# Score tiles of four heads on 32 rows, two token tiles to a unit, in three attention layers of a fused decoder (Trainium2, 1 core)

## What is computed

```python
h = (x - mean(x)) / sqrt(var(x) + eps)          # per token
q, k, v = h @ Wq + bq, src @ Wk + bk, src @ Wv + bv   # src is h (a1) or the context (x2, x3)
s = einsum('bhqd,bhkd->bhqk', q, k) / sqrt(8)   # 16 heads of width 8, 64 x 64 scores
w = softmax(s)                                  # x3: the denominator has one more term, exp(0)
x = x + (w @ v) @ Wo + bo                       # x3 has no Wo
```

## Time and profile before

| what | value |
|---|---|
| median of 3 runs | 2318.76 us (2318.24 to 2321.27) |
| profiled execution, its span | 2356.9 us; no other time is given for it |
| phase a1 | 728.9 to 908.2 us of the span |
| phase x2 | 1453.9 to 1618.7 us |
| phase x3 | 1897 to 2061 us |
| busy over the span | PE 1774.8 us, DVE 1337.8 us, ACT 1099.5 us, POOL 746.9 us |

### The profile page before, as it was taken

The page is one execution under the profiler, slowest core; times in us unless marked ns, Lnnn a source line. Parts: engine busy times, 40 slices in busy tenths (PEclk is TensorE's granted clock), DMA queues, the critical chain, the costliest instruction groups (busy, mean ns, idle before and its releaser), DMA issues. The chain is left out here.

```text
span 2356.9 us, 39525 instructions
## 1 busy us (share of the span) xinstructions
PE 1774.8 (75%) x14484; PEld 1215.4 (52%) x14484; DVE 1337.8 (57%) x3646; ACT 1099.5 (47%) x2273; POOL 746.9 (32%) x718
## 2 busy tenths in 40 slices
PE   3887553999895996767999386887788868743994
PEld 1555432435543664644798253565555535542774
DVE  3897587502123774654343365885369969862223
ACT  4775531223243775733344243774357657610441
POOL 1223201360354331146255002330223232165453
PEclk9888885798896998877999697998979969955997
DMA  4111361125623301102376200000000010011224
GB/s 158 83 83 82 104 235 45 49 75 150 161 70 132 124 2 50 37 30 85 110 238 201 75 1 27 28 20 10 3 1 2 2 37 28 11 49 60 62 81 138
DMA packets 145170, 173.18 MB, mean 73 GB/s; under 512 B 21073, under 2 KB 120593, under 8 KB 144049
## 3 DMA queue, kind: packets, MB, share of 16 engines
q1 hardware_dynamic: 125252, 129.09, 17.7%
q0 software_dynamic: 13248, 28.21, 3.6%
q10 hardware_dynamic: 6480, 13.37, 1.5%
HBM read 126.84 MB, written 79.05 MB: 87 GB/s over the span
## 5 line engine op out<-in xcount | busy, mean ns | idle before, releaser
L1154 PE MATMUL a_AV<-a_vx,a_pT 128*64 128x18 f32 (+1 forms) x3072 | 115.1, 224 | 33.0 <-DVE a_two L824 15.3
L1154 PEld LDWEIGHTS a_AV<-a_vx,a_pT 128*64 128x64 f32 x3072 | 105.9, 146 | 62.2 <-issue 28.6
L1016 ACT ACTIVATE a_e<-a_e 128x512 f32<-128x512 f32 x192 | 110.2, 622 | 58.7 <-DVE a_e L846 58.5
L1141 PE MATMUL a_TP<-ident,a_e 128*128 128x128 f32 x768 | 108.0, 285 | 20.0 <-ACT a_e L1016 19.4
L1021 ACT COPY a_pT<-a_TP 128x512 f32<-128x512 f32 x192 | 103.4, 588 | 39.6 <-PE a_TP L1141 39.4
L846 DVE TENSOR_TENSOR a_e<-a_S,a_mx 128x1024 f32<-128x1024 f32 x96 | 117.3, 1222 | 2.9
L1141 PEld LDWEIGHTS a_TP<-ident,a_e 128*128 128x128 f32 x768 | 89.2, 146 | 57.6 <-ACT a_e L1016 48.3
L1130 PE MATMUL a_S<-a_kbd,a_qT 64*64 64x512 f32 x768 | 113.8, 668 | 0.9 <-issue 0.6
L3620 POOL DMA_INDIRECT f_back<-f_ys,f_row x78 | 74.7, 957 | 97.5 <-DVE f_ys L3709 85.6
L3126 POOL DMA_INDIRECT f_back<-f_ys,f_row x80 | 76.6, 957 | 87.1 <-DVE f_ys L3287 66.9
L3759 ACT ACTIVATE f_h<-f_H,f_wt 128x256 f32<-128x256 f32 x156 | 65.2, 473 | 83.5 <-PE f_H L3835 83.5
(11 more groups left out here) (544 smaller groups left out, 4731.4 us busy)
## 6 DMA issues: line engine op xcount, KB each, us to landing
f_wt<-in_f_ew SPq DMA_DIRECT2D x39, 584.0 KB
f_slots<-in_blank SPq DMA_DIRECT2D x1, 18576.0 KB
f_wt<-in_f_leaf SPq DMA_DIRECT2D x94, 98.0 KB, 2.0
f_xs<-f_slots SPq DMA_DIRECT2D x47, 144.0 KB
memory_x_k<-w_stage ACTq DMA_DIRECT2D x24, 256.0 KB, 3.2
f_slots<-in_blank SPq DMA_DIRECT2D x1, 5760.0 KB
f_xs<-leaf_slots SPq DMA_DIRECT2D x22, 256.0 KB
leaf_out<-f_ys SPq DMA_DIRECT2D x22, 256.0 KB
```

The source lines that it names most:

```text
L1016: act.activation(eh, eh, ACT.Exp).then_inc(weights.sem, 1)
L1141: last = pe.transpose(TP[:, half, P * n:P * n + P], ev[:, 4 * half + n, :], k.ident[:, :])
L1154: last = pe.matmul(AV[64 * c:64 * c + 64, 2 * hp * W1:2 * (hp + 1) * W1], pT[:, hp, 64 * c:64 * c + 64], vx[:, g % 2, t, c, 2 * hp:2 * hp ...
```

## The change

A new function `attention_pairs` takes the place of `attention` in a1, x2 and x3; a0 and a3 keep the old one. Its program for VectorE puts `shift_mean(g + 2)` between the shifts of an even pair (in x3 `update` too) and `update` between those of an odd pair; behind the second shift stand `take_v(g + 1)` (even) and `norm_sums(g + 3)` (odd). Further:

- `score` uses 32 rows (four heads) in place of 64: eight matmuls per tile of 256 columns in place of four of 512, each of the four row strips r into its own bank.
- A score unit is two tiles (a pair p) and takes four banks, so there is one unit in place of two. `score(p + 1)` waits for both shifts of pair p.
- `highest` is one reduction of 2048 scores for two tiles; `shift` and `exps` stay per tile.
- The block-diagonal keys hold four heads per strip in place of eight, and GpSimd spreads all of them, in four instructions per group. ScalarE spreads none.
- `weigh` of both tiles of a pair writes one `AV` bank, and `take_values` takes both with one reciprocal and one product.

```diff
-    kbd = ph.sb("kbd", [P, 2, 2 * GT, 8, SL])
-    S = ph.ps("S", [P, 2, 2, 512])
+    kbd = ph.sb("kbd", [P, 2, 2 * GT, HR, SL])
+    S = ph.ps("S", [P, NR, 2, HR * SL])
...
+            def spread_keys(n):
+                wait_keys(pool, n)
+                if n >= 2:
+                    pool.wait_ge(scores.sem, scores.after(2 * (n - 2) + 1))
+                shape = [P, 2, HR, SL]
+                kb_ = keys(n).rearrange("p (b j) -> p b j", j=SL)
+                for b in range(0, 2 * GT, 2):
+                    last = pool.tensor_tensor(kbd[:, n % 2, b:b + 2, :, :], bc(kb_[:, b:b + 2, :], 2, shape),
+                                              mask4[:, :].unsqueeze(1).unsqueeze(3).to_broadcast(shape), ALU.mult)
+                last.then_inc(kbd_ready.sem, 1)
...
+            def shift(p, t):
+                if p:
+                    v.wait_ge(turned.sem, 2 * (2 * (p - 1) + t) + 2)
+                v.tensor_tensor(e[:, t, :, :].rearrange("p (r h) j -> p r h j", r=NR), S[:, :, t, :].rearrange("p r (h j) -> p r h j", j=SL),
                                bc(mx[:, p % 2, :, t, :], 3, [P, NR, HR, SL]), ALU.subtract).then_inc(shifted.sem, 1)
...
+            for p in range(NPR):
+                highest(p)
+                shift(p, 0)
+                if p:
+                    take_values(p - 1)
+                between(p)
+                shift(p, 1)
+                behind(p)
...
+            def score(p):
+                g, h = p // 2, p % 2
+                if h == 0:
+                    pe.wait_ge(q_ready.sem, q_ready.after(g))
+                    pe.wait_ge(kbd_ready.sem, kbd_ready.after(g))
+                if p:
+                    pe.wait_ge(shifted.sem, shifted.after(2 * (p - 1) + 1))
+                for t in range(2):
+                    for c in range(2):
+                        b = 4 * h + 2 * t + c
+                        for r in range(NR):
+                            rows = slice(32 * r, 32 * r + 32)
+                            last = pe.matmul(S[64 * c:64 * c + 64, r, t, :], qT[rows, g % 2, SL * b:SL * b + SL],
+                                             kbd[rows, g % 2, b, :, :], start=True, stop=True)
+                last.then_inc(scores.sem, 1)
...
+            for p in range(NPR):
+                g, later = p // 2, p // 2 + 2 < NG
+                turn(p, 0)
+                if p + 1 < NPR:
+                    score(p + 1)
+                weigh(p, 0)
+                if p == 0 and not cross:
+                    make_v(1)
+                elif p % 2 == 0 and g and finishing:
+                    ...
+                    turn_att(g - 1)
+                elif p % 2 and later:
+                    make_q(g + 2)
+                turn(p, 1)
+                if p % 2 == 0 and g and finishing:
+                    project(g - 1)
+                elif p % 2 and later and not cross:
+                    make_k(g + 2)
+                weigh(p, 1)
+                if p % 2 == 0 and later:
+                    if g and finishing:
+                        pe.wait_ge(x_updated.sem, x_updated.after(g - 1))
+                    ...
+                    turn_x(g + 2)
+                elif p % 2 and later and not cross:
+                    make_v(g + 2)
...
-            3: lambda: attention(nc, k, d, "a1", ...
-            7: lambda: attention(nc, k, d, "x2", ...
+            3: lambda: attention_pairs(nc, k, d, "a1", ...
+            7: lambda: attention_pairs(nc, k, d, "x2", ...
-           10: lambda: attention(nc, k, d, "x3", ...
+           10: lambda: attention_pairs(nc, k, d, "x3", ...
```

More of the change, by code:

```diff
@@ L3876, in shape_tables @@
     t["ident"] = np.eye(P, dtype=f)
+    t["mask4"] = ((p[:, None] // 8) % 4 == np.arange(4)[None, :]).astype(f) * f(8.0 ** -0.5)
     t["mask8"] = ((p[:, None] // 8) % 8 == np.arange(8)[None, :]).astype(f) * f(8.0 ** -0.5)
@@ L4035, in decoder @@
             0: lambda: attention(nc, k, d, "a0", "a0_q", "a0_k", "a0_v", "a0_o", width=16, diff=0.8 - 0.6 * 2.718281828459045 ** (-3.6), fill="f1"),
-            3: lambda: attention(nc, k, d, "a1", "a1_q", "a1_k", "a1_v", "a1_o", qb="a1_bq", kb="a1_bk", vb="a1_bv", ob="a1_bo", fill="f3"),
-            7: lambda: attention(nc, k, d, "x2", "x2_q", "x2_k", "x2_v", "x2_o", kv="ctx", qb="x2_bq", kb="x2_bk", vb="x2_bv", ob="x2_bo"),
+            3: lambda: attention_pairs(nc, k, d, "a1", "a1_q", "a1_k", "a1_v", "a1_o", qb="a1_bq", kb="a1_bk", vb="a1_bv", ob="a1_bo", fill="f3"),
+            7: lambda: attention_pairs(nc, k, d, "x2", "x2_q", "x2_k", "x2_v", "x2_o", kv="ctx", qb="x2_bq", kb="x2_bk", vb="x2_bv", ob="x2_bo"),
             9: lambda: attention(nc, k, d, "a3", "a3_q", "a3_k", "a3_v", "a3_o", qb="a3_bq", kb="a3_bk", vb="a3_bv", ob="a3_bo",
                                  affine=("a3_ga", "a3_be"), bias=True),
-            10: lambda: attention(nc, k, d, "x3", "x3_q", "x3_k", "x3_v", kv="ctx", qb="x3_bq", kb="x3_bk", vb="x3_bv",
+            10: lambda: attention_pairs(nc, k, d, "x3", "x3_q", "x3_k", "x3_v", kv="ctx", qb="x3_bq", kb="x3_bk", vb="x3_bv",
                                   restricted=True),
```

387 lines of the change are left out of this document (added).

## The result

The changed kernel takes 2350.45 us (median of four runs, 2345.37 to 2355.28) against 2320.02 (four runs, 2318.24 to 2330.38; the fourth came after the forecast): a ratio of 1.0117, 95% interval 1.0086 to 1.0147, so about 27 us slower. The forecast was 2341, in a range of 2294 to 2364, with 0.63 on slower.

What follows compares the result with a forecast made beforehand. TensorE was taken to bound a1 and VectorE x3. The shorter loop wins 12 + 5 + 5 = 22 us, clock falls lose 44: 22 us slower, put on the median as 2341 us, range 2294 to 2364.

Steps and rivals of the forecast that it cites:

- Score: TensorE in a1, x2, x3: a pair's score burst takes 1.05 us in place of 2 x 1.02; bounds 1.0 and 2.04.
- Maxima and values: VectorE, per pair: reduction of 2048 scores 2.3 us, reciprocal about 0.3, product 0.33; about 0.5 us saved.
- Loop at the full clock: Group lengths at unchanged clock: a1 16.8 us against 19.19, x2 16.8 against 17.79, x3 16.5 against 17.80.
- shift_mean 0.2: VectorE in a1's odd pair: shift_mean was counted at 0.2 us within a VectorE sum of 1.97.
- Clock: TensorE's clock falls in the new loop's long waits; PEclk by phase about 0.95 (a1), 0.90 (x2), 0.78 (x3).
- Price of a fall: Time lost to the low clock: a1 7 us (2 falls of 3.4), x2 15, x3 22, together 44 us.
- 5.5 more: x3: a group wholly at the low clock costs TensorE about 22.0 us against 16.5, so 5.5 us more.
- The ends: First group and drain of a1, x2, x3: 0, 0 and +1.5 us, bounds -3 and +4 in each.
- Slow strips: Rival: score's row strips do not run beside each other, 2.04 us a pair; 38 us slower, 2357; chance 0.10.
- The clock holds: Rival: no clock falls in the new loop, so 22 us faster, 2297 (2304 with up to two falls); chance 0.27.
- Nothing to see: Rival: clock falls and loop gain cancel within 5 us, 2319; chance 0.10.
- x3 longer, x2 a little longer, a1 shorter: Sign named for the forecast: x3 longer than its 163 us, x2 a little longer, a1 shorter than 179.

Runs made afterwards that it cites:

- the moved turn_x: Changed kernel with values taken behind both shifts and turn_x put behind the odd pair's score, no idle matmuls: 2289.49 us, ratio 0.9868.
- both fillers: Changed kernel plus idle matmuls ahead of each score burst and ahead of turn_x (in x3 after an odd pair's second weigh): 2314.55 us, ratio 0.9978.
- the runs: The change in a1 alone, x2 and x3 as in the kernel before: 2323.92 us, ratio 1.0014.
- the doubling: Changed kernel with every score matmul issued twice, the same result written again: 2370.73 us, ratio 1.0198.
- late values, moved turn_x and idle matmuls: Changed kernel, values behind both shifts, turn_x behind odd pair's score, idle matmuls in x3 and behind the first score burst of a1, x2, x3: 2271.85 us, ratio 0.9787.

## Why the prediction was right

**Sign and size.** 2341 was forecast, 2350 came. The mechanism is the one that was put first: the loop is shorter at the full clock, the clock falls in the new waits, and that costs more than the loop gains. The idle matmuls show it without changing any order, by 32 us. How near the total came is in part luck, as the parts show.

**Score.** 1.05 us a pair: exact. Eight quarter-height pieces do run side by side: a pair's 32 passes of 256 columns are 8192 columns, eight times the 1024 of a q projection's two passes, and those take 0.96 us.

**Maxima and values.** 2.3 for the reduction (2.29), 0.3 and 0.33 for reciprocal and product (0.36 and 0.42). Fine.

**Loop at the full clock.** 16.8, 16.8 and 16.5 were forecast. 17.90 came in a1 and 16.16 in x3; x2 has only the estimate of 16.4. So x2 and x3 are right to about half a microsecond. In a1 one term was mis-sized: "shift_mean 0.2" in the sum of the odd pair is 1.03 us (above), and it stands between take_values and the second shift, on the loop. The odd pair takes 9.29 us from score to score (814.73 to 824.02) where 8.5 was forecast. So five inner groups gain 5 x 1.29 = 6.5 us there, not 12.

**Clock.** PEclk of the inner stretches: about 0.95, 0.90 and 0.78 were named, and 0.90, 0.86 and 0.75 came. a1 has 27 us at the low clock there and not the 14 of two falls. Its busy share was worked out as 93%, near the 92% of before. It came as 85% in the group at the full clock (15.22 of 17.90 us), for the idle time of a group is 2.7 us in two waits, 1.51 before turn_x and 1.17 before score, and the forecast had only the first of them.

**Price of a fall.** In a1 a group at PEclk 0.91 has 3.5 us at the low clock and is 1.60 longer (19.50 against 17.90), near the half that the forecast took. The falls in its five inner groups cost 6.3 us in all (94.8 less 4 x 17.90 and the 16.82 of the fifth), against 7. "5.5 more" for a group of x3 wholly at the low clock holds too: the group from 1997.75, low for 13.6 of its 20.07 us, took 3.9 more than 16.16, which in proportion is 5.7 for a whole one (an estimate). The 1.76 us that the earlier trace rows gave for a fall in x3 was a reading against unlike groups, though: the one of 19.56 us has 16.12 us of VectorE's work and the others 17.04.

**The ends.** This is the step that was mis-sized most. They were put at 0, 0 and +1.5, with bounds of -3 and +4. By the traces they came as +6.8, +4.5 and +9.8 (table above), all outside the bounds, though the last of these holds falls that the sum had in its 22 for x3. The sum put nothing on a phase's start. The starts of a1 and x2 are 5.8 and 4.5 us longer at a lower PEclk. In the kernel with the moved turn_x two idle matmuls there gave 4.2 and 3.1 us back, so a good part of this is the clock's, as far as single traces tell (they differ by some 5 us in a1's start). How much the reduction of two tiles adds is not known. In x3 it is the last stretch, 12.5 us longer at PEclk 0.52; with both fillers it went from 40.2 to 33.5 us.

**What cancelled.** By phase -5, +10 and +17 were forecast, and the traces have +6.6, +11.2 and +10.2 (a1 is +3 by the runs). a1 was too low, by the loop gain of 12 in place of 6.5 and by the start. x3 was too high: its groups gained 1.64 us each at the full clock in place of 1.3, its start was 2.7 us shorter and not longer, and its falls took less than 22. The 11.8 us that came back there with both fillers are a lower bound of what they took, since a filled group at PEclk 1.00 takes 16.73 us against 16.16. Seven groups of that are 4 us more, so some 16 is an estimate. These errors have opposite signs, and that they nearly cancel in the total is luck.

**The rivals.** Slow strips: refuted by the trace and priced by the doubling. The clock holds: no, but the kernel with fillers is what this rival described, and it gives 2315 where 2297 was worked out; its fillers are in the way in a1, and the phase starts stay at the low clock. Nothing to see: no.

**x3 longer, x2 a little longer, a1 shorter:** two of three. (The 179 us named for a1 ends its phase at 908.2; from its first BN_STATS to the next phase's it is 183.4 before and 190.0 after.) And take_values is waited for, as it had to be.

## What to carry to other kernels

When work is taken from TensorE, look at the shape of the idle time that is left and not only at its amount: waits of 1 to 2 us between short pieces of work made the clock fall, and filling them gave back 12 to 14 us a phase where TensorE was on the path (x2, x3) and nothing that could be measured where it was not (a0). Look at the start and the drain of a phase too: 21 of the 28 us stood there. An idle matmul in the wait gives a lower bound of the clock's share in one run, lower by what the filler itself costs. Where a change gives up one of two buffer units, write the order on the engine that frees the other anew: with the values behind both shifts and turn_x behind score the same change is 31 us faster than before, with idle matmuls 49.

## What the runs showed of the hardware

**A 4-element instruction of 1.03 us.** shift_mean has the same shape everywhere and takes from 0.15 to 1.14 us in the rows here. GpSimd's timeline in a1 of the changed kernel beside it:

```profile
840.16 4.03 POOL L1342 TENSOR_TENSOR a_kbd<-a_kT,a_mask 128x512 f32<-128x512 f32 x4 [5.42 <-ACT a_kT L1518]
```

GpSimd is in the second of four key spreads of 1.01 us each when VectorE starts shift_mean at 841.18, and the spread ends at about 842.2, as shift_mean does (841.18 + 1.03 = 842.21). VectorE in x2 of the kernel with late values, moved turn_x and idle matmuls has both cases, and below them GpSimd's spreads and its bias:

```profile
1481.13 0.15 DVE L1383 SCALAR_TENSOR_TENSOR x_nmr<-x_mv,x_rstd 128x4 f32<-128x4 f32 x1
...
1495.57 1.14 DVE L1383 SCALAR_TENSOR_TENSOR x_nmr<-x_mv,x_rstd 128x4 f32<-128x4 f32 x1
```

```profile
1491.41 4.03 POOL L1342 TENSOR_TENSOR x_kbd<-x_kT,x_mask 128x512 f32<-128x512 f32 x4
1495.41 1.28 POOL L1350 TENSOR_TENSOR x<-x,rows 128x512 f32<-128x512 f32 x1
```

At 1481.13 GpSimd is idle and the instruction takes 0.15. At 1495.57 GpSimd is at its bias, which ends at 1496.69, and VectorE's ends at 1496.71. So in these rows a small VectorE instruction with both inputs in SBUF ends only with GpSimd's. The 0.79 of x2 before reads as the same wait. The Trainium skill, "SBUF — State Buffer", section "Who interferes with whom", says that a VectorE instruction with two SBUF inputs contends with a GpSimd one that reads SBUF, and that the port pair which the two share is an exclusive lock; these rows agree. That the two engines' instructions were only seen side by side is to be kept in mind: no run here took the key spreads away.

**The clock fell beside waits of 1.2 to 2.2 us**, with TensorE at work on both sides of them (rows above), and with both idle matmuls PEclk of the five inner groups was 1.00 in a1, 1.00 in x2 and 0.98 in x3 (0.93, 0.86 and 0.78 without them). A wait of that length doesn't bring a fall each time: the a1 group from 812.53 has two of them and ran at 1.00.

**A phase that starts at the low clock keeps it for a while.** In the kernels with the moved turn_x two idle matmuls behind the first score burst, where TensorE waits for the first exponentials, brought the stretch up to the first update from 60.7 to 56.5 us in a1 (PEclk 0.68 to 0.73) and from 50.0 to 46.9 in x2 (0.66 to 0.75). In a1 PEclk was 0.50 for the first 20 us of the phase in both; over the 10 us from 736.4 it was 0.59 without them, and over the 10 from 734.2 it was 0.98 with them.
